# Second cross attention of a gated two-layer block: attended values for two heads at a time from split operands, and two reordered stages

## The reference

```python
x = x + tanh(g_xattn[0]) * L0_xattn(layernorm(x), ctx)      # 16 query heads, 4 key/value heads of 128, keys = context
x = x + tanh(g_ffn[0])   * L0_ffn(layernorm(x))             # causal self attention, 16 heads, then 4 experts, top 2
x = x + tanh(g_xattn[1]) * L1_xattn(layernorm(x), ctx)      # the stage changed most
x = x + tanh(g_ffn[1])   * L1_ffn(layernorm(x))             # gated feed forward, ternary weights
```

```python
q = rope(rms_norm(x @ wq))            # 16 heads of 128
k = rope(rms_norm(x @ wk)); v = x @ wv            # 4 heads of 128, 256 keys, causal
k_ctx = rms_norm(ctx @ wk_ctx); v_ctx = ctx @ wv_ctx   # 4 heads, 64 keys, no mask
p = softmax(q @ concat(k_ctx, k).T / sqrt(128) + mask)
out = (p @ concat(v_ctx, v)) @ wo
```

## Time and profile before

| what | value |
|---|---|
| median of 3 runs | 1808.29 us (1808.27 to 1815.24) |
| the profiled execution's own time | 1810.08 us |
| its span, first to last instruction | 1808.3 us |
| busy over the span: PE, PEld | 1702.6 us (94%), 1546.0 us (85%) |
| busy: ACT, DVE, POOL | 1316.5 us (73%), 1103.2 us (61%), 1092.6 us (60%) |
| mean granted TensorE clock | 0.976 |
| opening | 0 to 54 us |
| first cross attention | 54 to 333 us |
| second cross attention | 1086 to 1688 us |

### The profile page before, as it was taken

How to read it: one execution, slowest core, us unless ns; L and a number is a source line. 1 busy time by engine, 2 the same in 40 slices (tenths; PEclk the granted TensorE clock), 3 DMA queues, 4 the chain that set the end, 5 groups by cost and what they waited for, 6 DMA issues and landing times.

```text
span 1808.3 us, 36021 instructions
## 1 busy us (share of the span) xinstructions
PE 1702.6 (94%) x11392; PEld 1546.0 (85%) x11392; DVE 1103.2 (61%) x3103; ACT 1316.5 (73%) x4275; POOL 1092.6 (60%) x1223
## 2 busy tenths in 40 slices
PE   5899998799999999999988978999999999999898
PEld 3788887698999999999977877898888888888897
DVE  4577768577766666667767784555555555565322
ACT  5677777598888888888855646888888888888311
POOL 4455546899998889899823134544444444554454
PEclk8899999899999999999989999999999999999998
DMA  4111201100000000000002100000000000000000
GB/s 141 53 41 34 69 27 59 36 19 13 25 13 19 19 19 13 19 13 19 13 32 72 29 11 15 9 8 12 9 12 8 13 9 18 14 18 11 9 19 24
DMA packets 32843, 45.90 MB, mean 25 GB/s; under 512 B 5264, under 2 KB 21904, under 8 KB 32656
## 3 DMA queue, kind: packets, MB, share of 16 engines
q1 hardware_dynamic: 32656, 43.59, 8.0%
HBM read 39.39 MB, written 4.19 MB: 24 GB/s over the span
## 4 chain that ended last, share of the span: by engine, by line
PE 62%; ACT 16%; DVE 7%; issue 7%; POOL 6%; DMA 1%; SPq 0%; POOLq 0%; DVEq 0%; ACTq 0%
PE pS L1106 4%; PE pF L292 4%; ACT pA L1670 4%; PE pF L294 4%; PE pF L293 4%; PE pA L292 3%; PE pA L294 3%; PE pA L293 3%; PE pA L621 3%; PE pA L622 3%; PE pA L623 3%; PE pO L1125 3%; PE pF L822 3%; ACT x_P L1892 3%; ACT x_P L1900 2%
## 5 line engine op out<-in xcount | busy, mean ns | idle before, releaser
L292 PE MATMUL pA<-Wh,XTh 128*128 128x512 f32 (+1 forms) x512 | 219.3, 428 | 5.0 <-DVE f_kT L1379 1.6
L1527 POOL TENSOR_TENSOR f_sw<-f_sw,f_sin 128x512 f32<-128x512 f32 x128 | 181.9, 1421 | 36.0 <-ACT f_sw L1236 36.0
L294 PE MATMUL pA<-Wh,XTl 128*128 128x512 f32 (+1 forms) x512 | 188.0, 367 | 0.0
L293 PE MATMUL pA<-Wl,XTh 128*128 128x512 f32 (+1 forms) x512 | 187.6, 366 | 0.0
L1236 ACT ACTIVATE f_sw<-pA 64x512 f32<-64x512 f32 x256 | 151.8, 593 | 34.6 <-PE pA L623 30.7
L1530 POOL TENSOR_TENSOR f_sw<-f_sw,f_RB 128x512 f32<-128x512 f32 x128 | 169.5, 1324 | 10.0
L287 POOL TENSOR_TENSOR Wl<-RAW,Wh 128x384 fp32r<-128x384 f32 (+3 forms) x72 | 75.6, 1050 | 165.4 <-ACT Wh L280 152.1
L621 PE MATMUL pA<-XTh,Wh 128*128 128x256 f32 x512 | 164.1, 320 | 5.3 <-DVE f_qT L1379 5.3
L1892 ACT ACTIVATE x_P<-x_P,x_nm 128x192 f32<-128x192 f32 (+1 forms) x256 | 127.9, 505 | 39.2 <-DVE x_nm L1977 39.2
L622 PE MATMUL pA<-XTl,Wh 128*128 128x256 f32 x512 | 145.9, 285 | 0.0
L623 PE MATMUL pA<-XTh,Wl 128*128 128x256 f32 x512 | 145.9, 285 | 0.0
(11 more groups left out here) (308 smaller groups left out, 6202.4 us busy)
## 6 DMA issues: line engine op xcount, KB each, us to landing
RAW<-in_w_f SPq DMA_DIRECT2D x32, 256.0 KB, 2.6
RAW<-in_w_x SPq DMA_DIRECT2D x32, 192.0 KB, 2.4
RAW<-in_w_x SPq DMA_DIRECT2D x32, 160.0 KB, 2.2
x_base<-in_w_x0b SPq DMA_DIRECT2D x20, 192.0 KB, 2.5
RAW<-in_w_ff SPq DMA_DIRECT2D x8, 288.0 KB, 2.7
R<-in_x SPq DMA_DIRECT2D x4, 512.0 KB, 7.1
x_spill<-R SPq DMA_DIRECT2D x8, 256.0 KB, 2.0
RAW<-in_w_moe SPq DMA_DIRECT2D x8, 256.0 KB, 2.6
```

The costliest lines, as they stand in the source:

```text
L292: e.matmul(o, ah, bh, start=first, stop=False)
L293: e.matmul(o, ah, bl, start=False, stop=False)
L294: return e.matmul(o, al, bh, start=False, stop=last)
L1527: e.tensor_tensor(y, y, bc(sind[:, :], 1, 2), ALU.mult).then_inc(q["swm"], 1)
```

## The change

In the second cross attention:

- `attend(i, hp)` does two heads at once (PR = 2 pairs a pass) with `three`: the transposed probabilities of a pair lie side by side as high part `PTh` and low part `PTl`, and so do `Vh` and `Vl`, `VSh` and `VSl`. It is 12 single matmuls: 3 of 512 columns, 9 of 2 x 128 columns, those written to two runs of the bank with a gap.
- `p_ev` now writes `PTh`; a new step `p_low` on VectorE writes `PTl` and counts `pl`. The next user of that `pT` bank waits for `pl` too (`bank_free`).
- `PTh`, `PTl`, `VSh` and `VSl` lie in spare columns of the weight slots `Wh[0]` and `Wl[0]`.
- `context_values` on GpSimd adds a copy (`VSh`) and a subtraction (`VSl`), each with a wait for the step before it; `VS` has one buffer. `rotate_k` on VectorE adds a subtraction for `Vl`. `take_kv` writes its squares to `tk`; `sk` is gone.
- `o_ev` and `o_low` do 512 columns twice a pass in place of 256 four times; `OTh` and `OTl` have three buffers of a pair.
- The hand-written orders change: TensorE has one attend behind `out_proj(i - 1, 0)` and one at the end of the pass, none behind `scores(i, 2)` or `out_proj(i - 1, 1)`; ScalarE and VectorE follow.

In the opening, VectorE's statistics run one more sequence ahead, and GpSimd does `norm.inverse(2)` ahead of `fold(0)`, and from chunk 1 on `low(c)`, `norm.inverse(c + 3)`, `fold(c + 1)` in this order. In the last pass of the first cross attention, `out_proj(i - 1)` and both `next_proj` come ahead of `p_tr(i)`.

```diff
@@ opening, dve
                 rows(1)
+                stats(2)
                 for b in range(B):
-                    if b + 2 < B:
-                        stats(b + 2)
+                    if b + 3 < B:
+                        stats(b + 3)
@@ opening, pool
                 inverse(2)
+                norm.inverse(e, 2)
                 fold(0)
                 inverse(3)
                 fold(1)
                 low(0)
-                for b in range(2, B):
-                    norm.inverse(e, b)
-                    fold(b)
-                    low(b - 1)
-                low(B - 1)
+                norm.inverse(e, 3)
+                for c in range(1, B):
+                    low(c)
+                    if c + 3 < B:
+                        norm.inverse(e, c + 3)
+                    if c + 1 < B:
+                        fold(c + 1)
@@ first cross attention, pe, last pass
                     else:
+                        out_proj(i - 1, 1 - s)
                         next_proj(0)
+                        next_proj(1)
                     p_tr(i)
...
-                    if not first:
+                    if not first and not last:
                         out_proj(i - 1, 1 - s)
...
-                next_proj(1)
                 out_proj(NI - 1, (NI - 1) % 2)
@@ cross_head
+            def bank_free(e, c):
+
+                e.wait_ge(q["te"], pos(c - 1))
+                if c >= 2 and turns[c - 2][0] == "p":
+                    e.wait_ge(q["pl"], HG * turns[c - 2][1] + turns[c - 2][2] + 1)
...
             def q_tr(e, i, t):
                 c = at_qk(i, t)
-                e.wait_ge(q["te"], pos(c - 1))
+                bank_free(e, c)
...
             def rotate_k(e, i):
...
+                ins = e.tensor_tensor(Vl[:, i % 3, :, :], x[:, :, 1, :], Vh[:, i % 3, :, :].bitcast(F32), ALU.subtract)
                 ins.then_inc(q["tk"], 1)
@@ cross_attention_1
+            AT = 8 * CW_X1
+            PTh, PTl = (x[0][:, AT:AT + 2 * 4 * P].rearrange("p (a n) -> p a n", a=2) for x in (Wh, Wl))
...
-                def attend(i, h):
-                    e.wait_ge(q["te"], at_p(i, h) + 1)
-                    e.wait_ge(q["ot"], HG * i + h)
-                    if h == 0:
-                        e.wait_ge(q["kv"], i + 1)
+                def attend(i, hp):
+
+                    m = PR * i + hp
+                    e.wait_ge(q["pl"], HG * i + 2 * hp + 2)
+                    e.wait_ge(q["ot"], m)
+                    if hp == 0:
+                        e.wait_ge(q["tk"], i + 1)
                         e.wait_ge(q["vs"], i + 1)
-                    e.matmul(pO[:, 0:S], V[:, i % 3, 0, :], PT[:, h % 2, P:P + S], start=True, stop=False)
-                    e.matmul(pO[:, P:S], V[:, i % 3, 1, :], PT[:, h % 2, P + S:2 * P + S], start=False, stop=False)
+                    o = pO[:, :].rearrange("p (a n) -> p a n", a=2)
+                    s, v = i % 2, i % 3
+                    three(e, o, Vh[:, v, 0, :], Vl[:, v, 0, :], PTh[:, :, P:P + S], PTl[:, :, P:P + S], True, False)
+                    three(e, o[:, :, P:S], Vh[:, v, 1, :], Vl[:, v, 1, :], PTh[:, :, P + S:2 * P + S],
+                          PTl[:, :, P + S:2 * P + S], False, False)
                     for t in range(T):
-                        ins = e.matmul(pO[:, t * P:(t + 1) * P], VS[:, i % 2, t, :], PT[:, h % 2, 0:P],
-                                       start=False, stop=(t == 1))
+                        ins = three(e, o[:, :, t * P:(t + 1) * P], VSh[:, s, t, :], VSl[:, s, t, :], PTh[:, :, 0:P],
+                                    PTl[:, :, 0:P], False, t == 1)
                     ins.then_inc(q["pv"], 1)
@@ pe, a pass
-                    attend(i, 0)
                     p_tr(i, 1)
                     scores(i, 3)
...
                     if i:
                         out_proj(i - 1, 0)
-                    attend(i, 1)
+                    attend(i, 0)
                     p_tr(i, 2)
...
                         out_proj(i - 1, 1)
-                    attend(i, 2)
...
-                    attend(i, 3)
+                    attend(i, 1)
@@ act
                 def p_ev(i, h):
                     c = at_p(i, h)
                     e.wait_ge(q["tr"], c + 1)
-                    e.wait_ge(q["pv"], pos(HG * i + h - 1))
-                    e.activation(PT[:, h % 2, :], pT[:, c % 2, :], ACT.Copy).then_inc(q["te"], 1)
+                    e.wait_ge(q["pv"], PR * i + h // 2)
+                    e.activation(PTh[:, h % 2, :], pT[:, c % 2, :], ACT.Copy).then_inc(q["te"], 1)
@@ dve
+                def p_low(i, h):
+                    c = at_p(i, h)
+                    e.wait_ge(q["te"], c + 1)
+                    e.tensor_tensor(PTl[:, h % 2, :], pT[:, c % 2, :], PTh[:, h % 2, :].bitcast(F32), ALU.subtract
+                                    ).then_inc(q["pl"], 1)
@@ dve, a pass
                     recip(i, 2)
-                    o_low(i, 0)
+                    p_low(i, 0)
+                    p_low(i, 1)
                     soft(i, 3)
                     if two:
                         rotate_k(e, k)
                     recip(i, 3)
...
-                    o_low(i, 1)
+                    o_low(i, 0)
+                    p_low(i, 2)
                     if i:
                         add_out(i - 1)
-                    o_low(i, 2)
...
                         recip(j, 0)
+                    p_low(i, 3)
+                    if one:
                         soft(j, 1)
...
-                    o_low(i, 3)
+                    o_low(i, 1)
@@ pool
                 def context_values(i):
...
+                    e.wait_ge(q["vsf"], i + 1)
+                    e.tensor_copy(VSh[:, i % 2], VS[:, :, :]).then_inc(q["vsh"], 1)
+                    e.wait_ge(q["vsh"], i + 1)
+                    e.tensor_tensor(VSl[:, i % 2], VS[:, :, :], VSh[:, i % 2].bitcast(F32), ALU.subtract
+                                    ).then_inc(q["vs"], 1)
```

More of the change, by code:

```diff
@@ L41 @@
 HB = B // 2
+PR = HG // 2
 NEG = -1e30
@@ L1562, in feed_up @@
             ins.then_inc(ff_up["gu"], 1)
-        Head = namedtuple("Head", "q QR qT kT V KR nrq at_p at_qk place proj_kv proj_q q_tr k_tr take_kv squares q_ev k_ev "
+        Head = namedtuple("Head", "q QR qT kT Vh Vl KR nrq at_p at_qk bank_free place proj_kv proj_q q_tr k_tr take_kv squares q_ev k_ev "
                           "take_q rotate_k context_keys inverse_norm_k sum_k sum_q inverse_norms_q t2")
@@ L1739, in inverse_norms_q @@
                 e.tensor_scalar(a, a, -1.0, None, ALU.mult).then_inc(q["rq"], 1)
-            return Head(q, QR, qT, kT, V, KR, nrq, at_p, at_qk, place, proj_kv, proj_q, q_tr, k_tr, take_kv, squares, q_ev,
+            return Head(q, QR, qT, kT, Vh, Vl, KR, nrq, at_p, at_qk, bank_free, place, proj_kv, proj_q, q_tr, k_tr, take_kv, squares, q_ev,
                         k_ev, take_q, rotate_k, context_keys, inverse_norm_k, sum_k, sum_q, inverse_norms_q, t2)
@@ L1747, in cross_attention_1 @@
             name = "x1"
-            (q, QR, qT, kT, V, KR, nrq, at_p, at_qk, place, proj_kv, proj_q, q_tr, k_tr, take_kv, squares, q_ev, k_ev, take_q,
+            (q, QR, qT, kT, Vh, Vl, KR, nrq, at_p, at_qk, bank_free, place, proj_kv, proj_q, q_tr, k_tr, take_kv, squares, q_ev, k_ev, take_q,
              rotate_k, context_keys, inverse_norm_k, sum_k, sum_q, inverse_norms_q, t2) = head
             NU, NT = 3, 3
+            AT = 8 * CW_X1
             OFF, WID = (0, SC + P), (SC + P, SC + S)
             WO = KD * (GW + 2 * HD)
-            VS = sb(name + "_VS", [P, 2, T, HD], F32, scope)
+            VS = sb(name + "_VS", [P, T, HD], F32, scope)
+            PTh, PTl = (x[0][:, AT:AT + 2 * 4 * P].rearrange("p (a n) -> p a n", a=2) for x in (Wh, Wl))
+            VSh, VSl = (x[0][:, AT + 8 * P:AT + 8 * P + 2 * T * HD].rearrange("p (s t n) -> p s t n", s=2, t=T)
+                        for x in (Wh, Wl))
             half = sb(name + "_half", [P, T], F32, scope)
@@ L1823, in norm_tr @@
                     c = place["norm", b]
-                    e.wait_ge(q["te"], c - 1)
+                    bank_free(e, c)
                     norm.turn(e, b, pT[:, c % 2, :]).then_inc(q["tr"], 1)
@@ L1935, in act @@
                         take_kv(e, k)
-                    o_ev(i, 0)
                     p_ev(i, 1)
@@ L1942, in act @@
                     exp(i, 3)
-                    o_ev(i, 1)
+                    o_ev(i, 0)
                     p_ev(i, 2)
@@ L1947, in act @@
                     normalise(i, 3)
-                    o_ev(i, 2)
                     w_high(i)
@@ L1960, in act @@
                         exp(j, 1)
-                    o_ev(i, 3)
+                    o_ev(i, 1)
                     if two:
```

52 lines of the change are left out of this document (28 added, 24 removed).

## The result

The changed kernel takes **1816.74 us** (median of 5 runs, 1813.98 to 1817.81), the kernel before 1808.29. The ratio is 1.0038, with a 95% interval of 1.0026 to 1.0050 (it is taken over all runs; the two medians alone divide to 1.0047): slower by a little, inside the 0.5% that I called no change. The forecast was 1810.4 within 1797 to 1824. The profiled executions are 1813.98 after (span 1812.2) and 1810.08 before (span 1808.3), 3.9 apart.

A forecast was written before the change was run, and what follows sets the result against it. A ring through ScalarE and TensorE bounds each second cross attention pass; 1810.08 + 6.3 (stage) - 4.2 (opening) + 0 (tail) = 1812.2 profiled, 1810.4 us for the runs, whose median lay 1.8 lower; range 1797 to 1824, likeliest case 1801 to 1817.

The forecast's parts named there:

- The ring: Second cross attention: a steady pass is a dependency loop, part ScalarE, part TensorE; 18.32 us becomes 18.70, +0.38 a pass.
- (a): TensorE, attend: one pair of 1.77 us replaces two attends of 2.20 in the ring, -0.43 us a pass.
- (b): ScalarE: o_ev at the ring's start evicts 512 columns, +0.22 us; o_ev(j,0) moves behind exp(j,3), -0.27.
- (c): VectorE: the p_low subtraction stands between p_ev(j,1) and the second q_tr, +0.72 us a pass, bounds 0.60 and 0.80.
- (d): Second path into the ring's start: the last pair's o_ev also waits for its attend, 4.67 against 4.53, +0.14 us.
- Passes 26 to 29: Second cross attention: norm_ev lengthens ScalarE's path and (d) falls away, so +0.24 us each, +1.0 in all.
- The last two passes: Second cross attention: without proj_kv and proj_q the attends weigh more, estimated at -0.9 us.
- Opening: Weight loading at the start: two chunks in flight, next stage starts at 50.1 against 54.28; -4.2 us, bounds -2 and -6.
- R1: Rival, faster: TensorE is the bound and its 27.5 us come off, 1776.6 us; chance 0.16 with its milder form.
- R2: Rival, slower: waits close together lower the granted clock, one spell a pass gives 1864 us; chance 0.09.
- R3: Rival, slower: strided output slows nine matmuls of each attend pair, 58 us, 1868 us; chance 0.04.
- R4: Rival, slower: each new link of the ring near its upper end, 0.6 to 0.8 a pass, 1817 to 1822 us; chance 0.11.

The follow-up runs named there:

- doubled subtraction: The changed kernel with p_low(i,1) issued twice in a row on VectorE: 1838.26 us, ratio 1.0164.
- two orders: The changed kernel with out_proj(i-1,0) behind both q_tr on TensorE, 1816.74 us, and with it issued ahead of them, 1777.75 us.
- both late: The changed kernel with out_proj(i-1,0) ahead of both q_tr, take_kv behind p_ev(i,1), squares(k,1) behind normalise(j,1) in passes 1 to 23: 1768.00 us.
- out first: The changed kernel with out_proj(i-1,0) issued on TensorE ahead of both q_tr: 1777.75 us, ratio 0.9833.
- the move: out_proj(i-1,0) issued ahead of both q_tr on TensorE, here in the kernel before: 1799.79 us, ratio 0.9957.

## Why the prediction was right, and where it was off

**The ring, and its sum of 18.70.** Right: 18.71 measured, term by term too. (a) From the second `q_tr` to the end of `proj_q(k,0)` it was 8.46 (1395.32 to 1403.78) and is 8.02 (1317.82 to 1325.84): -0.44 for the forecast -0.43. (b) From the start of the last pair's `o_ev` to `p_ev(j,1)` it was 4.68 and is 4.65: -0.03 for +0.22 - 0.27. (c) From `p_ev(j,1)` to the second `q_tr` it was 0.66 and is 1.42 (1316.40 to 1317.82): +0.76 for +0.72. (d) From the end of `proj_q(k,0)` to that `o_ev` it was 4.53 and is 4.62: +0.09 for +0.14. The doubled subtraction and the two orders show that (c) is in the ring with its full length, and which order puts it there. The profile calls the wait "issue" and not a wait for VectorE, as my list of signs had it; the doubling settles that.

`p_low` over all passes, one line's instructions:

```profile
L2010 DVE TENSOR_TENSOR Wl<-pT,Wh x128: 669/678/692, 1092.8 to 1684.2; 128x512 fp32r<-128x512 f32 x128
```

678 ns, exactly the neighbour that I took it from the earlier trace rows.

**Pass 0.** Right: -3.4 for -3.3. The one wait of 2.88 ahead of the first attend has become four, 0.44, 0.30, 0.56 and 0.07, and the granted clock is 1.00 from 1087 to 1107.

**Passes 26 to 29.** Mis-sized: +0.58 each for +0.24. I had (d) fall away there; the passes have the same waits ahead of `p_tr(j,1)` and both `q_tr` as the steady ones, the first `q_tr` waits 0.48 instead of 0.29, and nothing was taken off. Which step of ScalarE's order makes that 0.19 I did not try.

**The last two passes.** Wrong in sign: +0.9 for -0.9. The estimate counted attend work saved and forgot what a pair waits for. TensorE in order of time, the attends of the last passes:

```profile
1668.93 0.50 PE L293 MATMUL pO<-Wh,x_Vh 128*128 128x512 f32 x1 [2.73 <-DVE Wl L2010]
...
1684.95 0.65 PE L293 MATMUL pO<-Wh,x_Vh 128*128 128x512 f32 x1 [2.12 <-DVE Wl L2010]
```

Before, the attend of head 2 ran while head 3 was still in its softmax. The pair stands behind `p_low` of its later head, and then all of it lies at the end. There the last attend takes 3.42 (1684.95 to 1688.37, granted clock 0.53), and the last one of the kernel before 1.37 (from 1683.26, at 1.00, after a wait of 1.81). The clock doesn't make the sign, though: the kernel before has a stretch as long at the low level in the same two passes (1666.00 to 1669.40, 0.50), and the mean over them is 0.95 before and 0.96 after. Windows of the last attend, after and then before:

```profile
1684.95:1688.37 3.42, 3.42 (x12) 2.83 (x12) 0.00 (x0) 0.00 (x0) 0.07 (x1) 0.53 0.00 0
```

```profile
1683.26:1685.56 2.30, 1.37 (x8) 1.12 (x8) 0.42 (x1) 0.88 (x2) 1.02 (x1) 1.00 0.00 0
```

The order is read from the trace; no run took it apart.

**Opening.** The step held, a term was too big: the last weight DMA starts at 43.42 (forecast 43.7; the row of two ends at 43.75, and one issue is 0.33), `before` lands 2.60 after its issue (2.6), but from the last weights to the issue of `before` it is 2.74 (43.42 to 46.16), not the 3.76 of the kernel before. The issue of `be`, one of the small DMAs, took 1.37 there and takes 0.43 here. So the next stage starts 5.5 earlier, not 4.2. By the traces that reaches the second cross attention (1080.8 as the mean of nine, 1086.8 of four), but timed alone the opening gives 2.9 at the end. Where the rest goes in the median execution is open: the one profiled lost it in pass 0 and in the feed forward, at the low clock level. In the change pass 0 has no such stretch.

**First cross tail.** Right, by the trace and by the run of it alone.

**The sum.** For the profiled execution I had 1812.2, and it is 1813.98: opening -1.5, stage +3.7 (of it 1.3 in passes 26 to 29, 1.8 in the last two, 0.4 ahead of pass 0), feed forward -0.3. The other 4.5 us between 1810.4 and 1816.74 are in the step from that execution to the median: I took 1.8 off, as in the kernel before, and in the changed kernel the median lies 2.8 above the profiled one. So the time lies in the range, but 6 us above the forecast and near the top of its likeliest case, and part of that fit is luck. The term that decides, the stage, was too small: +6.3 forecast, +9.9 by the table, +13.2 timed alone. The steady passes, 9.5 of it, were right; passes 26 to 29 and the last two were not.

**The rivals.** R1 (TensorE is the bound) fell as the change stands, and is what happens in "both late", where 1768 even beats its 1776.6 (with TensorE's and ScalarE's orders changed too, which R1 didn't have). Its milder form, `p_low` out of the ring, is "out first": I priced it at 0.34 off a pass, and it is 0.87 (18.33 to 17.46), of which 0.42 is what the move gives without the change (17.91). R2 (the clock falls in the steady passes) fell: 1.00 over them, with three waits of up to 0.57 in each; the stretch at the low level in the last attend (0.64 over the 4.70 us shown) follows a single wait of 2.12, while the attend after 2.73 at 1668.93 ran at 1.00. So in these traces the length of the last wait alone doesn't tell whether the clock falls. R3 (strided output) fell: nine matmuls of a pair with two runs of 128 columns take 0.12 each. TensorE in order of time, the three kinds of a pair's matmuls:

```profile
1328.51 0.39 PE L293 MATMUL pO<-Wh,x_Vh 128*128 128x512 f32 x1
1328.74 0.39 PE L294 MATMUL pO<-Wl,x_Vh 128*128 128x512 f32 x1
...
1329.55 0.28 PE L293 MATMUL pO<-Wh 128*128 128x256 f32 x1
1329.67 0.28 PE L294 MATMUL pO<-Wl,Wh 128*128 128x256 f32 x1
```

Each starts 0.23 or 0.12 after the one before it, as with contiguous outputs. The Trainium skill (PSUM — Partial Sum Buffer, Specifications (TRN2)) says that any non-contiguous access pattern slows matmuls significantly; the trace doesn't agree for this one, whose runs are 128 fp32 elements long. R4 (each link near its upper end) fell in the steady pass, though the median came out near its 1817 by other terms.

## What to carry to other kernels

When work is cut on an engine that the chain shows inside a ring, sum the ring, not the engine: here some 27 us of TensorE work went (64 pairs by 0.43) and the kernel got slower, since a subtraction of 0.68 us was put between a bank's eviction and its next user. Before giving such a change up, look for work of the bound engine that depends on neither, and issue it in that gap: one moved block gave 39 us. And of the waits that the trace showed on TensorE, only the last one before the ring's next hand-over was worth moving something for; where one instruction takes over two users, it also waits for the later of them. Last, a time in the range doesn't make every term right: time the parts one by one, here +13.2, -2.9 and 0 for the forecast +6.3, -4.2 and 0.

## What the runs showed of the hardware

A wait on TensorE costs more than its idle time. In the table the TensorE work of the eight kernels with the change is the same (16.88 without a wait), but the time that isn't idle is 17.10 with one wait a pass, 17.28 and 17.44 with two and 17.43 and 17.49 with three: some 0.2 us for each wait (0.18 to 0.28) is booked as busy. Part of it is seen directly: four transposes take 0.60 without a wait ahead of them and 0.66 with one, and eight `q_tr` transposes 1.03 in one go, but 1.26 as two fours that each waited. The rest is in how a record is made: the next instruction starts 0.44 after such a group of four, inside its 0.60, and behind a wait that overlap of 0.16 is lost. An estimate from these rows, 0.16 + 0.06, is 0.22 a wait. So the 0.20 of idle time in the kernel before was worth 0.42 a pass.

The 0.5% between the kernels is smaller than what the low clock level moves about. The kernel before and the opening alone have the same second cross attention, but the 32 matmuls after the wait for `VS` ran at 0.72 and 0.60, the last two passes at 0.95 and 1.00, and the first 20 us of the feed forward at 1.00 and 0.83. The feed forward takes 121.4 to 125.8 us over the 13 traces with the same code. So a gain of a few us ahead of such places isn't sure to arrive, and a single pair of traces can't place it; the length of a steady pass can, to 0.02 us.
